# Self attention: V rows that carry their own one, one V transfer, stores of 17 rows, half the masks on VectorE

## What is computed

```python
q = q * cos + _rotate_half(q) * sin
k = k * cos + _rotate_half(k) * sin
scores = jnp.einsum('bhqd,bhkd->bhqk', q, k) * scale      # 16 heads of 16
causal = jnp.triu(jnp.ones((S, S), bool), k=1)
scores = jnp.where(causal, -jnp.inf, scores)
attn = jax.nn.softmax(scores, axis=-1)
out = jnp.einsum('bhqk,bhkd->bhqd', attn, v)
```

## Time and profile before

| what | value |
|---|---|
| median of 3 runs | 2710.33 us (2708.35 to 2712.96) |
| profiled execution, its own time | 2703.97 us |
| its span in the profile | 2702.2 us |
| PE, DVE, ACT, POOL busy over the span | 94%, 67%, 54%, 27% |
| causal `attention`, first to last matmul | 1652.8 to 1942 us |

### The profile page before, as it was taken

How to read it: one execution, slowest core, us unless ns; L and a number is a source line. 1 busy time by engine, 2 the same in 40 slices (tenths; PEclk the granted TensorE clock), 3 DMA queues, 4 the chain that set the end, 5 groups by cost and what they waited for, 6 DMA issues and landing times. The chain is left out here.

```text
span 2702.2 us, 46967 instructions
## 1 busy us (share of the span) xinstructions
PE 2527.6 (94%) x14109; PEld 1287.0 (48%) x14110; DVE 1807.6 (67%) x3818; ACT 1457.7 (54%) x2975; POOL 734.1 (27%) x1306
## 2 busy tenths in 40 slices
PE   8997999999999999999999896999773999999996
PEld 5665233333333333333332563444363777777774
DVE  5665888888888888888884696888565232233331
ACT  3343277777777777777778454777651222222221
POOL 5443000000000000000000585666563233333332
PEclk9999699999999999999999998999885999999998
DMA  6779643444433444433431588999684121211223
GB/s 196 245 225 248 90 55 57 62 70 69 69 54 57 64 70 69 68 53 56 66 45 44 163 248 162 180 183 178 154 249 120 28 32 33 33 32 32 34 33 83
DMA packets 486611, 270.82 MB, mean 100 GB/s; under 512 B 307312, under 2 KB 452736, under 8 KB 486240
## 3 DMA queue, kind: packets, MB, share of 16 engines
q1 hardware_dynamic: 460096, 234.43, 42.9%
q0 software_dynamic: 16192, 30.45, 6.0%
q10 hardware_dynamic: 10144, 3.75, 0.7%
HBM read 172.45 MB, written 99.50 MB: 101 GB/s over the span
## 5 line engine op out<-in xcount | busy, mean ns | idle before, releaser
L984 DVE TENSOR_REDUCE att_cross_neg_max<-att_cross_ps_s 128x1 f32<-128x401 f32 x2048 | 1027.6, 567 | 154.2 <-PE att_cross_ps_s L903 151.6
L1078 ACT ACTIVATE att_cross_probs<-att_cross_ps_st 128x512 f32<-128x512 f32 (+1 forms) x1664 | 879.8, 601 | 293.3 <-PE att_cross_ps_st L922 280.7
L903 PE MATMUL att_cross_ps_s<-att_cross_k_pack,att_cross_q_pack 96*128 96x401 bf16 x2048 | 656.4, 343 | 10.6 <-DVEq L970 10.1
L922 PE MATMUL att_cross_ps_st<-att_cross_q_pack,att_cross_k_pack 99*128 99x512 bf16 (+1 forms) x1664 | 630.9, 382 | 10.2 <-ACT att_cross_probs L1078 4.7
L937 PE MATMUL att_cross_ps_o<-att_cross_probs,att_cross_v_tiles 128*32 128x512 f32 (+1 forms) x3328 | 443.0, 605 | 0.1
L903 PEld LDWEIGHTS att_cross_ps_s<-att_cross_k_pack,att_cross_q_pack 96*128 96x128 bf16 x2048 | 201.3, 98 | 371.0 <-DVE att_cross_neg_max L984 242.2
L1026 POOL CAST att_cross_neg_max_parts<-att_cross_neg_max_merged 128x16 bf16<-128x16 f32 x32 | 6.3, 196 | 1139.8 <-DVE att_cross_neg_max_merged L977 1139.8
L922 PEld LDWEIGHTS att_cross_ps_st<-att_cross_q_pack,att_cross_k_pack 99*128 99x128 bf16 (+1 forms) x1664 | 163.9, 99 | 307.9 <-ACT att_cross_probs L1078 191.7
L984 DVE TENSOR_REDUCE att_self_neg_max<-att_self_ps_s 128x1 f32<-128x512 f32 (+3 forms) x512 | 226.2, 485 | 54.2 <-PE att_self_ps_s L906 47.2
L2145 DVE COPY moe_hiddenT<-moe_ps_h 128x256 f32<-128x256 f32 x142 | 60.2, 424 | 268.6 <-PE moe_ps_h L2041 268.6
L1078 ACT ACTIVATE att_self_probs<-att_self_ps_st 128x256 f32<-128x256 f32 (+3 forms) x512 | 199.1, 439 | 61.2 <-PE att_self_ps_st L922 58.9
(11 more groups left out here) (220 smaller groups left out, 2863.0 us busy)
## 6 DMA issues: line engine op xcount, KB each, us to landing
att_cross_k_pack<-k_parts SPq DMA_DIRECT2D x32, 600.4 KB, 6.9
k_parts<-in_part SPq DMA_DIRECT2D x72, 256.0 KB, 3.8
att_cross_k_pack<-k_parts SPq DMA_DIRECT2D x32, 400.2 KB, 9.1
in_rows<-in_ctx_dram SPq DMA_DIRECT2D x24, 512.0 KB, 4.7
v_rows<-in_v_biased SPq DMA_DIRECT2D x24, 512.0 KB, 4.0
att_cross_v_tiles<-v_rows SPq DMA_DIRECT2D x128, 96.0 KB
out_rows<-att_cross_out_buf SPq DMA_DIRECT2D x32, 256.0 KB, 10.4
out_rows<-att_self_out_buf SPq DMA_DIRECT2D x32, 256.0 KB, 4.4
```

What stands on the lines that cost most here:

```text
L903: mm = nc.tensor.matmul(ps_s[bank][:, 0:w], qp[v.buf][0:SROWS, j, q * P:(q + 1) * P], kp[v.buf][0:SROWS, j, s:s + w], start=True, stop=not ...
L922: mm = nc.tensor.matmul(ps_st[bank_of_step[s]][0:rows, q0:SEQ], kp[u.buf][0:MROWS, j, t * P:t * P + rows], qp[u.buf][0:MROWS, j, q0:SEQ], ...
L984: nc.vector.tensor_reduce(nmax[v.odd][:, j * QT + q, i:i + 1], ps_s[bank][:, 0:w], AX.X, ALU.max, negate=True).then_inc(s_read, 1)
L1078: nc.scalar.activation(pr[0:rows, (u.odd * STEPS + s) % RING, q0:SEQ], ps_st[bank_of_step[s]][0:rows, q0:SEQ], ACT.Exp).then_inc(exp_done, 1)
```

## The change

V of the self attention is kept in device memory with 17 columns a head (`VO` = 17), the last of them ones, which `project_self` sets once in its tile `vs`. `load_v` then needs one transfer a unit where it needed four (one a head), and the V tiles are 17 columns wide instead of 32; POOL no longer sets ones and zeros in them. The product matmuls write 17 rows a head, and DVE clears `ps_o` once. `send_out` stores for each head its 17 used rows, in four transfers, where one transfer stored all 128 rows. Of the masks, those of the pieces of 128 and 256 keys stay with PE; for those of 384 and 512 keys DVE adds the mask (`later`) and reduces in one call, `tensor_tensor_reduce`.

```diff
@@ Packs.load_v
+        if self.causal:
+            src = self.v_rows[v.batch, :, v.heads.start * VO:v.heads.stop * VO]
+            eng.dma_start(self.va[self.vbuf(v)][:, :, :, :].rearrange("p t j w -> p t (j w)"),
+                         src.rearrange("(t p) v -> p t v", p=P)).then_inc(self.v_in[self.vbuf(v)], 16)
+            return
@@ attention
-        VLOADS = 16 * GH * ((1 if kv >= P else 0) + (1 if kv % P else 0))
+        VLOADS = 16 if causal else 16 * GH * ((1 if kv >= P else 0) + (1 if kv % P else 0))
+        def masked_by_pe(w):
+            return causal and w <= 2 * P
@@ send_out
-                    sp.dma_start(out_rows[v.n, :, :], ob[v.odd][:, :]).then_inc(o_sent[v.odd], 16)
+                    if causal:
+                        for j in range(GH):
+                            used = slice(j * VW, j * VW + VO)
+                            sp.dma_start(out_rows[v.n, used, :], ob[v.odd][used, :]).then_inc(o_sent[v.odd], 16)
@@ PE, maxima and products
-                                              kp[v.buf][0:SROWS, j, s:s + w], start=True, stop=not causal)
-                        if causal:
+                                              kp[v.buf][0:SROWS, j, s:s + w], start=True, stop=not masked_by_pe(w))
+                        if masked_by_pe(w):
-                        nc.tensor.matmul(ps_o[j * VW:(j + 1) * VW, q0:SEQ],
+                        nc.tensor.matmul(ps_o[j * VW:j * VW + packs.vw, q0:SEQ],
@@ DVE
+                    nc.vector.memset(ps_o[:, :], 0.0).then_inc(o_read, 1)
+                    nc.vector.memset(later[:, 0:SEQ - P], 0.0).then_inc(later_set, 1)
+                    nc.vector.tensor_copy(later[:, SEQ - P:SEQ], keep["mask_q"]).then_inc(later_set, 1)
+                    if causal and not masked_by_pe(w):
+                        nc.vector.tensor_tensor_reduce(ps_s[bank][:, 0:w], ps_s[bank][:, 0:w], later[:, SEQ - w:SEQ],
+                                                       -1.0, 3.0e38, ALU.add, ALU.min, to).then_inc(s_read, 1)
@@ project_self
-        vs = p.sb("v_rows", [P, QT, DIM])
+        vs = p.sb("v_rows", [P, QT, HEADS, VO])
+                nc.gpsimd.memset(vs[:, :, :, HD:VO], 1.0).then_inc(v_one_set, 1)
```

More of the change, by code:

```diff
@@ L42 @@
 VW = 32
+VO = HD + 1
 class Prog:
@@ L581, in __init__ @@
         self.vbufs = 4 if causal else 2
+        self.vw = VO if causal else VW
+        self.ones = 0 if causal else 2 * self.vbufs
         self.kp, self.qp = [], []
@@ L584, in __init__ @@
             self.add_pack(self.p)
-        self.va = [self.p.sb(f"v_tiles{i}", [P, -(-kv // P), GH, VW]) for i in range(self.vbufs)]
+        self.va = [self.p.sb(f"v_tiles{i}", [P, -(-kv // P), GH, self.vw]) for i in range(self.vbufs)]
         self.ones_set = self.p.sem("ones_set")
@@ L606, in set_early_ones @@
         pool.wait_ge(self.ones_set, early)
-        for va in self.va:
+        for va in () if self.causal else self.va:
             self.nc.gpsimd.memset(va[:, :, :, HD + 1:VW], 0.0).then_inc(self.ones_set, 1)
             self.nc.gpsimd.memset(va[:, :, :, HD:HD + 1], 1.0).then_inc(self.ones_set, 1)
-        pool.wait_ge(self.ones_set, early + 2 * self.vbufs)
+        pool.wait_ge(self.ones_set, early + self.ones)
     def load_kq(self, eng, v):
@@ L638, with __init__ @@
 class Denominators:
-    def __init__(self, nc, p, stage, out_rows, den, inv):
+    def __init__(self, nc, p, stage, out_rows, den, inv, stores):
+        self.out_sent = 16 * stores
         self.nc, self.den, self.inv = nc, den, inv
@@ L883, in _ @@
                 send_out(Unit(units // 4 - 1, 3))
-                shares.last_count = 16 * (units // 2 + 1)
+                shares.last_count = OUT_SENT * (units // 2 + 1)
             @block.tensor
@@ L1004, in _ @@
                 nc.gpsimd.memset(nm_parts[:, 3:, :], 0.0).then_inc(ones_set, 1)
-                pool.wait_ge(ones_set, BUFS - late + 2 * VBUFS + 1)
+                pool.wait_ge(ones_set, BUFS - late + packs.ones + 1)
                 packs.set_ones(pool, BUFS - late, BUFS)
-                pool.wait_ge(ones_set, BUFS + 2 * VBUFS + 1)
+                pool.wait_ge(ones_set, BUFS + packs.ones + 1)
                 LINKS = 3
@@ L1067, in _ @@
                 act.sem_inc(exp_done, 3)
-                act.sem_inc(o_read, 1)
+                if not causal:
+                    act.sem_inc(o_read, 1)
                 act.sem_inc(m_rows_in, 1)
```

37 lines of the change are left out of this document (25 added, 12 removed).

## The result

The changed kernel takes 2749.8 us (median of 4 runs, 2749.3 to 2755.2) beside 2711.6 us for the kernel before in the same comparison. The ratio is 1.0146, with a 95% interval of 1.0134 to 1.0158: slower by 38 us.

The account below looks back on a forecast made before the run. PE bounds the kernel at 8.65 us a unit; after the change one DMA engine does, at 10.2. Units +42 and -2, end +5, start +1: +46 us, 2750 profiled, 2756 median beside 2710.33; range 2718 to 2798.

Parts of the forecast that it names:

- one step: Output stores: 17 rows go as one share, so every unit's four stores run on the same first DMA engine; chance 0.84.
- The sign that it leaned on: DMA view: 65-row V store and maxima show no landing time, read as transfers on fewer than 16 engines; no size.
- Rival 1: Output stores spread over engines, DMAs have room: unit 8.17 to 8.35 us, total 2697 to 2702 us; chance 0.11.
- Rival 2: Stores spread or cheap, DVE's second instruction costs 0.24 us, PE stops 0.46 us at the transpose: about 2709 us; chance 0.05.
- The unit, 10.2 us: Causal stage: the one DMA engine's work sets the pace, 10.2 us a unit (9.3 to 11.6) in place of 8.65.
- the bytes-only bound: The one DMA engine's unit time by bytes alone: 224 KB at 24 GB/s, 9.3 us.
- the sum of packet times: The one DMA engine's packets priced by size and added: 11.6 us a unit, 10.6 allowing for overlap; stores 6.8 of it.
- The start, +1 us: Start of the causal stage: DVE's reads in the first maxima, 8 x 0.1, cost +1 us.
- The end, +5 us: Stage's end: last stores queue on one engine, 6.8 us against one store's landing, plus leftovers of the unit before: +5 us.
- The masks' 0.48 us: PE: eight of a unit's 16 mask matmuls go, 0.06 us each, saving 0.48 us a unit, hidden behind the DMA engine.
- a = 0.10: DVE: added time of each masked reduction, 0.06 to 0.24 us, taken as 0.10, giving DVE 7.2 us a unit.
- The point from which the stores decide: One DMA engine: with under about 40 of the 68 stored rows its sum falls below 8.6 us a unit.

Follow-up runs that it names:

- e2: Changed kernel with 18 rows in place of 17 in each of its four stores: 2706.1 us, ratio 0.9988 to the kernel before.
- e3: Changed kernel with 32 rows in place of 17 in each of its four stores: 2706.7 us, ratio 0.9986 to the kernel before.
- e6: Kernel before with only the masks of 512 and 384 moved to DVE: 2711.7 us, ratio 1.0000.
- e1: Changed kernel with the unit's output stored as one transfer of all 128 rows again: 2707.9 us, ratio 0.9992 to the kernel before.
- e7: Changed kernel with two stores of 17 rows and one of 64 in place of four of 17: 2732.6 us, ratio 1.0076 to the kernel before.
- e12: e2 with SP holding the V loads of units 1 and 2 and the fourth pack until the first maxima land: 2703.9 us, ratio 0.9974.
- e8: e1 with SP holding the V loads of units 1 and 2 and the fourth pack until the first maxima land: 2701.9 us, ratio 0.9965.
- e11: Changed kernel with its four 17-row stores held until the next unit's maxima have landed: 2786.4 us, ratio 1.0276 to the kernel before.
- e4: Kernel before with the four 17-row stores and nothing else of the change: 2765.7 us, ratio 1.0226.

## Why the prediction was right

**The mechanism.** The forecast hung on one step: 17 rows can't be shared out, so four such stores load one DMA engine. It held (e2, e3), and that it is one engine for all four the packet records show: 19 packets in a row at 6.6% of 16 engines. The sign that it leaned on, the missing landing time of a 65-row store and of the maxima, was a weak one: e2's stores have none either. The last share of V lands 2.3 us later than without them. That SP's queue is pushed back by full rings, as the prediction has it, no run shows. Rival 1 (stores spread) is what e2 measures: 0.9988, 2706 us, not 2697 to 2702. Rival 2 (the second DVE instruction) is refuted by its price.

**The unit, 10.2 us.** Right in kind, too high in size: 9.60 in units 10 to 29, against bounds of 9.3 and 11.6. 224 KB in 9.60 us is 23.3 GB/s, so the bytes-only bound was the nearer one. I leaned to the sum of packet times, each of which counts time that overlaps: a store's packet was priced at 0.10 us and the records start one every 0.08, 5.4 us for 68 in place of 6.8. I also let the full loss begin after two units; the first ten took 9.13. So the units gave +23.5 us in place of 42 - 2.

**The start, +1 us.** Wrong: +5.0. I priced DVE's part at 1 and e6 has 1.0, but in part by luck: half of that goes with the clock (0.76), which I left unchanged. I did not price that four issues of V becoming one moves the loads behind them forward, in front of the first maxima, nor that PE then starts on the unit at a granted clock of 0.70 where it had 1.00 (1.2 us). A transfer that is cheaper to issue is not only cheaper.

**The end, +5 us.** +6.3. At the stage's end SP needs 8.91 us for the last two units' stores.

**The total.** +46 for a profiled execution, by luck also its difference of 45.9; by the medians 38. What I had too much in the units (16 us) was in part offset by too little at the start (4) and the end (1); the other 11 of the 45.9 lie outside the stage (6.7 ahead of it, 4.4 behind), where the forecast had nothing. 2756 to 2749.8, within the range.

**PE.** 89% busy, not 80 to 85, because the units are shorter than forecast. The masks' 0.48 us: an undisturbed unit went from 8.55 to 8.25 (e1), 0.30. The rest is the stop at the transpose (0.13, forecast up to 0.18) and one of 0.08 at the scores behind a 384, about the 0.18 that are missing. 8.35 was expected as likeliest.

**DVE.** a = 0.10 was too high: 0.02 and 0.04 us from start to start. The second instruction's 0.14 us lies beside the next one's start.

**The point from which the stores decide.** I put it at about 40 of 68 rows. Wrong: at 38 rows the loss is 0.76%. The sum of work was the wrong test below the full dose; the maxima's transfer has 5.3 us to land and needs 6.6 when a third of it shares the stores' engine. In e7 that third starts 1 us after the others are done and is drawn out to 1.4 us by taking turns with the stores' packets; why it starts so late stays open. How much of after's 1.1 us a unit (9.44 against 8.30 in e1) is the sum and how much this wait is open too.

## What to carry to other kernels

Before you cut a store to its used rows, look at how many equal shares the row count allows: 68 rows in four transfers of 17 cost 1.5%, 72 rows in four of 18 nothing. A load that becomes cheap to issue comes earlier, and what is small and urgent then waits behind it; one wait in the issuing queue gave back 0.1 to 0.3% (e2 to e12, e1 to e8). And a DMA engine can cost time below its capacity, if a small transfer that everything waits for passes through it.

## What the runs showed that I had not expected

- Four stores of 17 rows hold SP for 4.1 to 5.1 us a unit in after, where four of 18 rows take 1.8 to 2.4 us (e2) and one of 128 rows 0.35 to 0.8 (e1); the same four take 1.3 us in e11 and 1.9 to 2.2 in e4.
- A 12 KB transfer takes 3.95 us from issue to use both at a DMA share of 0.33 (e8) and at 0.95 in packets of 64 bytes (e6), 7.20 with V and the fourth pack issued just ahead of it (e1), and 6.6 to 6.75 with 38 rows of 2 KB on one engine in each unit.
- DVE's masked reduction costs 0.02 to 0.04 us more than the plain one, though it shows as 0.70 + 0.14 us.
- The granted clock isn't a matter of the busy share alone: from 1690 to 1925 us it was 0.91 in e11, where PE was busy 86%, and 1.00 in e4, where it was 87%. After's 0.98 comes from its first 9 us (0.60) and from 1700 to 1725 us (0.93); from 1725 us on it was 1.00 with PE 89% busy.
